# Layer 0 of a two-layer megakernel: the inverse roots of five groups' input variances, computed by VectorE's Newton steps instead of a GpSimd power

## The reference, cut to what matters

```
x = x + ga * _L0_attn_ref(h, ...)
h = _layernorm(x, axis=-1) * (1 + cb) + sb          # (x - m) / sqrt(v + eps)
x = x + gb * _L0_ffn_ref(h, L0_ffn_Wg, L0_ffn_bg, L0_ffn_W1, L0_ffn_W2, L0_ffn_W3)
# in _L0_ffn_ref:
gate_logits = xt @ Wg + bg
top_v, top_i = jax.lax.top_k(gate_logits, TOPK)
seq = jnp.cumsum(expert_label, axis=0) * expert_label   # slot in the expert's queue
```

## Time and profile before

| | us |
|---|---|
| median of 3 runs | 839.18 (839.06 to 839.41) |
| the profiled execution, its own time | 838.07 |
| its span, first to last instruction | 836.7 |
| PE busy in the span | 799.2 (96%) |
| DVE busy | 604.1 (72%) |
| ACT busy | 434.5 (52%) |
| POOL busy | 395.0 (47%) |
| layer 0, up to the end of the last send | about 159 of the span |

### The profile page before, as it was taken

How to read it: one execution, slowest core, us unless ns; L and a number is a source line. 1 busy time by engine, 2 the same in 40 slices (tenths; PEclk the granted TensorE clock), 3 DMA queues, 4 the chain that set the end, 5 groups by cost and what they waited for, 6 DMA issues and landing times.

```text
span 836.7 us, 32664 instructions
## 1 busy us (share of the span) xinstructions
PE 799.2 (96%) x13828; PEld 699.4 (84%) x13828; DVE 604.1 (72%) x1779; ACT 434.5 (52%) x942; POOL 395.0 (47%) x399
## 2 busy tenths in 40 slices
PE   6999987899998899999999999999999999989998
PEld 5777767799997688888888888888898889878887
DVE  7898887567545766675777776786867777768865
ACT  6556634344544746566566565575665654523322
POOL 4348887425454735643646646447443434400000
PEclk9999999999999999999999999999999999999999
DMA  9814141233413000000100000200000000048751
GB/s 282 285 45 181 41 134 26 76 94 116 131 48 110 27 3 4 28 4 4 53 4 4 29 4 3 55 4 3 4 3 4 4 4 3 3 87 158 150 117 38
DMA packets 67904, 49.66 MB, mean 59 GB/s; under 512 B 5343, under 2 KB 62774, under 8 KB 67376
## 3 DMA queue, kind: packets, MB, share of 16 engines
q1 hardware_dynamic: 64288, 42.41, 18.8%
q0 software_dynamic: 3328, 5.16, 1.9%
q10 hardware_dynamic: 144, 0.02, 0.0%
HBM read 33.20 MB, written 16.10 MB: 59 GB/s over the span
## 4 chain that ended last, share of the span: by engine, by line
PE 72%; POOL 9%; DVE 6%; issue 5%; DMA 4%; ACT 3%; SPq 1%; DVEq 0%; POOLq 0%; ACTq 0%
PE psum L1625 16%; POOL disp L312 7%; PE psum L1730 7%; PE psum L1755 7%; PE psum L1781 7%; PE psum L2421 5%; PE psum L1299 5%; PE psum L1692 5%; PE psum L2439 4%; PE psum L1770 4%; PE psum L1672 3%; PE psum L1644 3%; PE psum L1335 3%; POOL sb_l_y L231 2%; DMA sb_e_x<-disp 1%
## 5 line engine op out<-in xcount | busy, mean ns | idle before, releaser
L2320 POOL TENSOR_TENSOR sb_a_qr<-sb_h,sb_a_csq 128x512 f32<-128x512 f32 x64 | 81.0, 1287 | 92.1 <-PE psum L1755 88.2
L1625 PE MATMUL psum<-sb_wkv,sb_a_hs 128*128 128x512 f32 (+1 forms) x414 | 122.1, 407 | 1.0 <-ACT sb_a_hs L2108 0.7
L2320 POOL TENSOR_TENSOR sb_a_qr<-sb_a_qp,sb_a_csq 128x512 f32<-128x512 f32 (+1 forms) x64 | 72.2, 1150 | 94.9 <-PE psum L1755 94.9
L1916 ACT ACTIVATE sb_a_vr<-sb_a_va,sb_consts 128x520 f32<-128x520 f32 x128 | 86.6, 726 | 14.4 <-DVE sb_a_va L2178 14.1
L312 POOL DMA_INDIRECT disp<-sb_h,sb_slot x64 | 68.4, 1069 | 23.4 <-issue 18.1
L1625 PEld LDWEIGHTS psum<-sb_wkv,sb_a_hs 128*128 128x128 f32 x414 | 66.0, 190 | 12.5 <-ACT sb_a_hs L2108 0.9
L1730 PE MATMUL psum<-sb_a_mid,sb_a_qr 64*64 64x65 f32 x2048 | 70.6, 218 | 0.0
L1755 PE MATMUL psum<-sb_a_vr,sb_a_kb 64*64 64x130 f32 x1920 | 70.5, 272 | 0.0
L2199 DVE TENSOR_TENSOR sb_a_mid<-psum,sb_a_state 128x130 f32<-128x130 f32 x112 | 47.3, 422 | 26.5 <-PE psum L1755 26.4
L1229 POOL DMA_INDIRECT chosen<-sb_m_h3t,sb_e_row x40 | 39.3, 983 | 57.1 <-ACTq L1413 42.4
L2178 DVE TENSOR_TENSOR sb_a_va<-psum,sb_rows 128x512 f32<-128x512 f32 x64 | 44.0, 688 | 30.6 <-PE psum L1625 30.6
(11 more groups left out here) (292 smaller groups left out, 1983.1 us busy)
## 6 DMA issues: line engine op xcount, KB each, us to landing
sb_h<-turned SPq DMA_DIRECT2D x32, 256.0 KB, 5.5
sb_e_w<-in_w SPq DMA_DIRECT2D x24, 256.0 KB, 3.2
chosen<-sb_empty SPq DMA_DIRECT2D x8, 512.0 KB, 6.4
sb_a_g<-chosen SPq DMA_DIRECT2D x12, 256.0 KB, 3.3
disp<-sb_empty SPq DMA_DIRECT2D x4, 650.0 KB, 9.9
sb_e_x<-disp SPq DMA_DIRECT2D x7, 325.0 KB, 5.0
sb_a_wo<-in_wo SPq DMA_DIRECT2D x4, 512.0 KB, 4.2
out<-sb_x SPq DMA_DIRECT2D x7, 256.0 KB, 3.9
```

The lines of the kernel that those rows point to most:

```text
L1625: ins = self.pe.matmul(out[:, x * w:(x + 1) * w], stationary, moving[:, x * w:(x + 1) * w], start=(k == 0 and x == 0), stop=(k == 2), skip ...
L1916: ins = act.activation(self.Vr[i % 2][:, :, k, :], self.Va[i % 3][:], ACT.Copy, scale=self.c[("cos1", "sin1")[k]][:, n:n + 1])
L2320: ins = g.tensor_tensor(self.Qr[i % 2][:, k, :, t], qp, rows(self.csQ[:, k, c * P + t.start:(c + 1) * P], PH), ALU.mult)
```

## The change

The GpSimd function `input_roots` and its five calls, in iterations it = 1 to 5, are gone. `last_root` becomes `newton_root(c, between)`, for any group, and VectorE calls it at the head of iterations 1 to 5 with nothing to put between the steps. `input_means(c)` moves up with it, so that `outputs_gated(g)` now stands behind both. The two joint powers, the output powers and the last group's root stay where they were; the last group's call is the old function under its new name.

```
-    def input_roots(self, c):
-        S = self.S
-        self.pool.wait_ge(S["ln3"], c + 1)
-        self.pool.wait_ge(S["l0_xn3"], c)
-        self.inverse_root(self.y3[:], self.t3[:]).then_inc(S["l0_root3"], 1)
-
...
         for it in range(NGRP - 2):
-            if it:
-                self.input_roots(it - 1)
             self.dispatch(3, it - 2)
             self.output_roots(it)
...
-    def last_root(self, between):
+    def newton_root(self, c, between):
 
         v, S, vs, t, y, h = self.dve, self.S, self.vs, self.t3[:], self.y3[:], self.h3[:]
-        v.wait_ge(S["ln3"], NGRP)
-        v.wait_ge(S["l0_xn3"], NGRP - 1)
+        v.wait_ge(S["ln3"], c + 1)
+        v.wait_ge(S["l0_xn3"], c)
         v.tensor_scalar(h, t, -0.5, None, ALU.mult)
         k = vs.did(v.tensor_scalar(y.bitcast(I32), t.bitcast(I32), -0.5, MAGIC, ALU.mult, ALU.add))
         for n in range(3):
-            next(between)
+            next(between, None)
             v.wait_ge(vs.sem, k)
             k = vs.did(v.tensor_tensor(t, y, y, ALU.mult))
...
             if g < 2:
                 self.keys_stats(3 + 2 * g)
+            if c >= 0:
+                self.newton_root(c, iter(()))
+                self.input_means(c)
             self.outputs_gated(g)
-            if c >= 0:
-                self.input_means(c)
             self.keys_rotated(a)
...
-        self.last_root(labels)
+        self.newton_root(NGRP - 1, labels)
```

## The result

| | before | after |
|---|---|---|
| median | 839.29 (837.17 to 840.27, 6 executions) | 845.20 (842.46 to 846.25, 6) |
| ratio | | 1.0069, 95% interval 1.0047 to 1.0092 |
| profiled execution, its own time | 838.07 | 844.63 |
| its span | 836.7 | 843.3 |

In a later session the changed kernel came out at 845.02 (7 executions) against 839.13 (18): ratio 1.0060, 1.0039 to 1.0081. The sign and the mechanism were as forecast, the size was not: +5.9 us, above the upper end of 844.0.

What follows compares the result with a forecast made beforehand. Layer 0 was bound by the loop through VectorE and TensorE, not GpSimd; delays of 1.32 + 1.00 + 0 + 1.00 + 0 = +3.3 us at the first joint power carry to the end: 842.5, range 840.9 to 844.0.

Steps and rivals of the forecast that it cites:

- Where the time goes, and the sign: Layer 0: iterations 1, 2, 4 cost +1.32, +1.00, +1.00, iterations 3 and 5 nothing; GpSimd not the bound; slower, 0.87.
- The Newton chain at 0.20 a distance: VectorE's heads: dependent steps 0.20 apart, ends 0.16 and 0.24; `t3` to the mean's predecessor L986 2.34 in sum.
- +3.3 at the joint power: First joint power, GpSimd, layer 0: starts 3.3 us later, at about 119.3 instead of 116.00.
- Where TensorE waits: Layer 0: idle before the transposes rises from 0.69 to about 1.7 in iterations 2 and 4, near none in 3, 5.
- TensorE's durations in the sum: Path to the joint power and on: only delays 1.32 + 1.00 + 0 + 1.00 + 0 added; no clock term.
- the shift goes to the end of the kernel: Behind the first joint power: the path stays as before and the whole +3.3 reaches the end, TensorE being at 96%.
- The range: Whole kernel: 840.9 to 844.0, from the second-lowest end considered up to the forecast's 843.6 plus the runs' spread of 0.35.
- The third rival: VectorE's heads, iterations 2 to 5: each running send holds a Newton step for 0.97; +6.3, 845.5; 4 in 100.

Runs made afterwards that it cites:

- The kernel with two wide products and the old list length: Changed kernel plus two unread 128x512 TensorE products before the gated-output wait in iterations 1, 2, 4, six spare products removed ahead of the experts: 843.98, ratio 1.0053.
- The four kernels without a fall: Changed kernel plus unread TensorE products: six small in iterations 1, 2, 4 (874.16) or 2 (845.77); two 128x512 in 1, 2, 4 (853.41), or with six spare removed (843.98).
- steps in 3 and 5: Changed kernel with Newton steps on VectorE only at heads 3 and 5; iterations 1, 2, 4 keep GpSimd's power and the old order: 839.51, ratio 0.9988.
- the three with all three idle times filled: Changed kernel plus unread TensorE products in iterations 1, 2, 4: six small each (874.16), two 128x512 each (853.41), or those two with six spare products removed (843.98).
- the run with six products in iteration 2: Changed kernel plus six unread 128x128 identity products before TensorE's gated-output wait in iteration 2, six later spare products removed: median 845.77, ratio 1.0075, profiled 840.25.
- 18 small products (three places): Changed kernel plus six unread 128x128 identity products before TensorE's gated-output wait in each of iterations 1, 2 and 4: 874.16, ratio 1.0389.
- Three wide ones: Changed kernel plus one unread 128x512 TensorE product before the gated-output wait in each of iterations 1, 2 and 4: 846.86, ratio 1.0087.

## Why the prediction fell short, point by point

- **Where the time goes, and the sign: right.** The heads of iterations 1, 2 and 4 cost, 3 and 5 don't, GpSimd isn't the bound, the joint powers wait for VectorE and carry the delay to the last send.
- **The Newton chain at 0.20 a distance: right.** 0.20 measured, `t3` to L978 2.26 and 2.49 where 2.34 was forecast. The gating follows the mean after 0.18 (63.97 to 64.15), not 0.08.
- **+3.3 at the joint power: right where the clock stays up.** The kernel with two wide products and the old list length shows no fall in layer 0's heads (and VectorE has no idle time before the old L932 and L992 in iteration 2, as was forecast); its ScalarE copies of the turned tiles stand +1.1 behind those of before in iteration 1, +2.3 in 2 and 3, +3.2 in 4 and 5, and its joint power at +3.17. The four kernels without a fall have 118.86 to 119.36.
- **Where TensorE waits: half right.** The idle time was forecast ahead of the transposes, at 1.7. It stands ahead of L504, at 1.86 and 1.62, since the gated output now comes behind the mean; the transposes follow 1.0 behind. Both paths take the same 1.9 from L978, so the sum was not touched. What I did not ask is what one long idle time in place of two short ones does to TensorE.
- **The step that failed: TensorE's durations in the sum.** The sum took every duration of the trace of before as given, in the "+3.3 us at the first joint power" and in "the shift goes to the end of the kernel". What the longer idle times do to TensorE's granted clock is a term that it put at nothing, without a reason. The joint power of the changed kernel came 4.62 late with one fall ahead of it and 7.43 late with three, and 2.9 to 3.4 late in the four kernels without one. The idle times in the heads were 0.7 to 0.8 us before (with one of 0.35 ahead of it in iteration 1) and are 1.6 to 2.5 now. Of the profiled executions, the five with steps in all five heads and nothing put into the idle times had ten falls ahead of the joint power, each at least one; the three with short idle times (before, twice, and steps in 3 and 5) had one, and the three with all three idle times filled had none.
- **What it comes to.** The account of the two medians: 3.2 of delay and 2.7 for 2.1 more falls of 1.3, together 5.9, against 5.6 measured (845.06 less 839.44; the means differ by 5.1). Execution by execution it is an estimate: both profiles of the changed kernel have five falls over the span, three more than the first of before, which makes 3.2 + 3.9 = 7.1, and their spans are 6.6 and 7.0 longer. The 840.25 of the run with six products in iteration 2 doesn't fit as well: 3.1 of delay and one more fall make 4.4, and its span is 2.2 longer. The Trainium skill, "TensorE: Matmul & The Clock Gate", section "HAM oscillation — how this bites in real kernels", describes this way to lose time, products that wait and then start at the low clock. The rows at 49.83 and 64.89 agree with that; the waits of the page's example are longer than the 2.46 and 1.86 here.
- **The range.** It took the spread of three executions, 0.35, for that of the kernel. Over 62 executions before goes from 836.5 to 843.6. The trace of before had a fall at 136 and one at 262. The page's row of granted clocks shows tenths of wide slices and hides them; windows of 2 us over the span show them. Two more of them at 1.3 each would have put the upper end at 846.6, and the measured 845.2 inside.
- **The third rival** (steps held by the sends, 845.5) gives nearly the measured time, and is wrong: beside running sends the steps keep their 0.16 and the sends their 0.97. What is seen is small: a multiplication that starts together with a send takes 0.20 (62.17), and one `t3` takes 0.38 (61.48) and ends together with the send that began at 60.88. The Trainium skill's rule in "SBUF — State Buffer", section "Summary: rules for kernel authors", by which one of the two blocks fully, is not seen here in either direction. The rival's price was right by chance; only the rows tell the two apart.

What stays open: which idle times bring a fall. In one execution the clock fell at 48 behind 0.81 us of idle time, in the three others profiled with the same idle time there it held; in the changed kernel 2.47 at 47 brought none in the first profile and a double one in the second. At 126 in the changed kernel and at 120 in the second profile of before, the last idle time, 0.82, had ended about 2 us before the fall. It is a matter of how often, and 13 executions bound that roughly. What one fall costs is an average too; with its 3.17 at the joint power and 0.5 falls more (0.7), the kernel with two wide products and the old list length should lie 3.9 over the 839.13 of its session, and lies 4.9 over it. Why TensorE stalls in layer 1 when its list is longer was not separated from where in memory the list then lies. No form beat the kernel of before: with steps only in 3 and 5 the interval is 0.9969 to 1.0007.

## What to carry to other kernels

Before moving work onto an engine that TensorE waits for, read TensorE's idle times and not only the path: here a wait that grew from 0.7 to some 2 us cost its length and, in part of the executions, about 1.3 us more for a fallen clock. Price that, and read the spread of executions from their mean granted clocks rather than from three times that happen to agree. A chain of dependent small instructions on VectorE cost its number times 0.20 us here, 2.3 us for a root that GpSimd gave in 1.3, and belongs only where the consumer is busy anyway.

## What the runs showed of the hardware

- Dependent VectorE instructions of 128x4 follow each other at 0.197 us, though each is 0.16 long; in the old root, with routing work between them, it was 0.24 (1.95 for eight).
- A fall of TensorE's granted clock from 1.00 to 0.50 takes 1.7 us of full clock (single) and comes at other places in each execution; over 61 executions of the kernel before, its time moves by about 1.3 us with it.
- Adding 18 small products (three places) in layer 0 costs 28 us in a loop of layer 1, in 23 stalls of about 1.2 us. Three wide ones show 4.6 us of such waits, six 10.9, six with as many others taken out ahead of layer 1 1.7, and the changed kernel without any 1.3. So whoever adds products to this kernel has to read "issue" in TensorE's waits.
